# A graph block with experts: weight preparation in the first block, experts' weights behind index loads

## The chip, the cores and the metric

The kernel runs on one core of a Trainium2 chip. The metric is the device time of one execution in microseconds. The hand-written program gives TensorE (PE), VectorE (DVE), ScalarE (ACT), GpSimd (POOL) and SyncE (SP) their own instruction lists, which meet only at semaphores. SP, ACT and GpSimd also issue DMAs: SP's go through queue q1, ACT's through q10, GpSimd's through q0, and all run on the core's 16 DMA engines.

## The reference

One layer over a graph with 6250 nodes of 256 features and 100,000 edges sorted by destination, all in float32:

```python
def gat_conv(x, src, dst, W, a_src, a_dst, b):
    h = (x @ W).reshape(-1, H, C)
    alpha_s = einsum('nhc,hc->nh', h, a_src)
    alpha_d = einsum('nhc,hc->nh', h, a_dst)
    e = leaky_relu(alpha_s[src] + alpha_d[dst], 0.2)
    m = segment_max(e, dst)
    ex = exp(e - m[dst])
    alpha = ex / (segment_sum(ex, dst)[dst] + 1e-16)
    return segment_sum(h[src] * alpha[:, :, None], dst).reshape(-1, H * C) + b
xn = layernorm(x)
x = x + gat_conv(relu(gat_conv(xn, ...W1...)), ...W2...) + linear_attention(xn, Wqkv, Wout, bout)
x = x + experts(layernorm(x), gate_w, w1, w2, ...)      # 16 experts, the best 2 of each node
```

Self-loops are added to the edges. The attention normalises keys and values over each head's 64 features before their product, and its result is one 256 by 256 matrix applied to every node.

## The kernel before

The program is a row of stages, each with its own semaphores, ended by a barrier of all engines: `prepare_edges`, `project_inputs`, `bounds`, `maxima`, `gat_edges` (first layer), `bounds`, `maxima`, `gat_edges` (second layer), `order`, `experts`, `finish`. Nodes go in 49 tiles of 128, edges in 98 chunks of 1024 (8 per partition).

`prepare_edges` (L229) copies the list of sources to `srcp`, and loads the destinations twice: as `dst_i` (L274), where every partition takes eight neighbouring integers of each chunk, so 32 bytes at a time, and as `by_chunk_i` (L276), 97 whole chunks of 4 KB each on a partition of its own. VectorE waits for these loads (L303) and then makes from them, step by step (L304 to L356), the codes that say to which window and which node an edge belongs. SP stores the codes at L279.

`project_inputs` (L368) has two blocks. In the first, SP issues nine loads of weights (L399 to L407: W1, W2, four attention vectors broadcast to all partitions, the key and value weights of 1 MB, the query and output weights of 512 KB each); all add to one semaphore, and VectorE (L416) and TensorE (L437) wait for all nine. VectorE then appends the attention columns to W1 and W2 (L541, L542), copies six groups of four transposes that TensorE makes in one PSUM tile, `psW` (L424, L426), and takes the mean per head from the key and value weights (L431 to L433). In the second block x is loaded (L461), normalised, turned and multiplied with W1, tile by tile.

`gat_edges` (L761) is the edge stage. SP loads a chunk's sources (`idx`, three slots, L885) and its codes, broadcast to all partitions (`codes`, two slots, L889); GpSimd gathers the chunk's 1024 rows of the table in eight indirect DMAs into one of three slots (L931), once TensorE has added up what was in the slot (`added`, L929); VectorE makes the one-hot matrices (L971, L988), logits (L982 to L984) and scales the rows with ACT's exponentials (L995); TensorE adds up (L1215). `chunks` (L843) writes such a loop with an offset for each step; the code loads run one chunk ahead. In SP's list this gives: codes 0, idx 0, codes 1, idx 1, codes 2, idx 2. Codes 2 wait until VectorE has made the one-hot of chunk 0 (L888). At the start of the stage VectorE multiplies the self-loops' terms with their weights (L960), four long instructions. In the second layer ACT first issues three loads of four experts' weights each, 2 MB a load, into `w1` (L1162, L1163), which the later stages need (`weights_in`); the last four experts' come in `order`.

Of the kernel before, what the change touches and what calls it, by code (L numbers as in the profile page):

```python
# [25 lines left out]
P = 128  # L26
# [109 lines left out]
def build(nc, a, out):  # L136
# [15 lines left out]
    with ExitStack() as top:  # L152
# [27 lines left out]
        with ExitStack() as gnn:  # L180
# [26 lines left out]
            edges = (codes_d, partition, iota, acc, own, peak, parts, windows)  # L207
            stage(prepare_edges, a, srcp, codes_d, partition, ident, identb, ones, iota, eps, code, lower, upper, first_tile, passes)
# [19 lines left out]

def prepare_edges(nc, a, srcp, codes_d, partition, ident, identb, ones, iota, eps, code, lower, upper, first_tile, passes, sem):  # L229

# [3 lines left out]
    with ExitStack() as ctx:  # L234
        def sb(name, shape, dt=F32):
            return ctx.enter_context(nc.sbuf_tensor(name, shape, dt))
# [23 lines left out]
        count_i = sb("count_i", [1, 1], I32)  # L260
        base = sb("base", [P, 2, NC])
        ps = ctx.enter_context(nc.psum_tensor("pe_ps", [P, 512], F32))
        ps2 = ctx.enter_context(nc.psum_tensor("pe_ps2", [P, 512], F32))
        s = {n: sem("e_" + n) for n in ("filled", "loaded", "stored", "consts", "steps", "turned", "rowed", "spread", "tiled", "zeroed", "coded")}
        block = ctx.enter_context(nc.Block())
# [28 lines left out]
        def _(dve):  # L294
# [6 lines left out]
            dve.tensor_copy(partition[:], partition_i[:])  # L301
            dve.tensor_copy(identb[:], ident[:])
            dve.wait_ge(s["loaded"], 64)  # L303
            dve.tensor_copy(code[:], dst_i[:])  # L304
# [51 lines left out]
            chain.link(dve.scalar_tensor_tensor(code[:], code[:], SPREAD, residue[:], ALU.mult, ALU.add))  # L356

        @block.tensor
        def _(pe):
            pe.wait_ge(s["consts"], 1)  # L360
            pe.wait_ge(s["tiled"], 1)
# [6 lines left out]
def project_inputs(nc, a, xnT_d, table, ident, eps, acc, dtab, dotsT, wkvT, wq, woutT, wext1, sem):  # L368

    with ExitStack() as ctx:  # L370
        def sb(name, shape, dt=F32):
            return ctx.enter_context(nc.sbuf_tensor(name, shape, dt))
# [3 lines left out]

        wext = sb("wext0", [P, 2, HW])
        att = sb("att0", [P, 2, C])
        attw = sb("attw0", [P, 2, C])
        att1 = sb("att1", [P, 2, C])  # L380
        wkv = sb("wkv", [P, 8, C])
        wmean = sb("wmean", [P, 2 * MH])
        wout = sb("wout", [P, 2, MI])
        x = sb("x_in", [P, BUFS, C])
# [6 lines left out]
        psH = pb("psH", [P, 2, 512])  # L391
        psW = pb("psW", [P, 512])
        loaded, steps, turned, moved = sem("i_loaded"), sem("i_steps"), sem("i_turned"), sem("i_moved")
        first_block = ExitStack()
        block = first_block.enter_context(nc.Block())

        @block.sync
        def _(sp):
            sp.dma_start(wext[:, :, 0:C], a["L0_gnn_W1"].rearrange("(k p) n -> p k n", p=P)).then_inc(loaded, 16)  # L399
            sp.dma_start(att[:, 0, :], a["L0_gnn_att_src1"].rearrange("(o h) c -> o (h c)", o=1).to_broadcast([P, C])).then_inc(loaded, 16)  # L400
            sp.dma_start(att[:, 1, :], a["L0_gnn_att_dst1"].rearrange("(o h) c -> o (h c)", o=1).to_broadcast([P, C])).then_inc(loaded, 16)
            sp.dma_start(wext1[:, :, 0:C], a["L0_gnn_W2"].rearrange("(k p) n -> p k n", p=P)).then_inc(loaded, 16)
            sp.dma_start(att1[:, 0, :], a["L0_gnn_att_src2"].rearrange("(o h) c -> o (h c)", o=1).to_broadcast([P, C])).then_inc(loaded, 16)
            sp.dma_start(att1[:, 1, :], a["L0_gnn_att_dst2"].rearrange("(o h) c -> o (h c)", o=1).to_broadcast([P, C])).then_inc(loaded, 16)
            sp.dma_start(wkv[:], a["L0_mix_Wqkv"][MI:3 * MI, :].rearrange("(k p) c -> p k c", p=P)).then_inc(loaded, 16)
            sp.dma_start(wq, a["L0_mix_Wqkv"][0:MI, :].rearrange("(k p) c -> p k c", p=P)).then_inc(loaded, 16)
            sp.dma_start(wout[:], a["L0_mix_Wout"].rearrange("(k p) c -> p k c", p=P)).then_inc(loaded, 16)  # L407

        @block.vector
        def _(dve):  # L410
            chain = Chain(dve, steps)
            dve.memset(acc[:, NT:NT + 2, :], 0.0)
            dve.memset(acc[:, NT + 2, :], 1.0)
            dve.memset(dtab[:, NT:NT + 3, :], 0.0)
            dve.memset(dotsT[:], 0.0)
            dve.wait_ge(loaded, 144)  # L416
            attention_columns(dve, chain, wext, att, attw)
            attention_columns(dve, chain, wext1, att1, attw)

            for g in range(6):  # L420
                dve.wait_ge(turned, g + 1)
                if g < 4:
                    kc, q = g // 2, g % 2
                    dve.tensor_copy(wkvT[:, kc, q, :], psW[:, :]).then_inc(moved, 1)  # L424
                else:
                    dve.tensor_copy(woutT[:, :, (g - 4) * P:(g - 3) * P], psW[:, :].rearrange("p (k f) -> p k f", k=4)).then_inc(moved, 1)  # L426

            dve.wait_ge(moved, 6)
            for kc in range(2):
                w = wkvT[:, kc, :, :].rearrange("p a (g d) -> p (a g) d", d=MD)  # L430
                chain.link(dve.tensor_reduce(wmean[:], w, AX.X, ALU.add))  # L431
                chain.link(dve.tensor_scalar(wmean[:], wmean[:], 1.0 / MD, None, ALU.mult))
                chain.link(dve.tensor_tensor(w, w, wmean[:].rearrange("p (g d) -> p g d", d=1).to_broadcast([P, 2 * MH, MD]), ALU.subtract))  # L433

        @block.tensor
        def _(pe):
            pe.wait_ge(loaded, 144)  # L437
            for g in range(6):
                if g:
                    pe.wait_ge(moved, g)  # L440
                for j in range(4):
                    if g < 4:
                        kc, q = g // 2, g % 2
                        ins = pe.transpose(psW[:, j * P:(j + 1) * P], wkv[:, 4 * q + j, kc * P:(kc + 1) * P], ident[:])
                    else:
                        ins = pe.transpose(psW[:, j * P:(j + 1) * P], wout[:, g - 4, j * P:(j + 1) * P], ident[:])
                ins.then_inc(turned, 1)
# [5 lines left out]
        block2 = ctx.enter_context(nc.Block())  # L453

        @block2.sync
# [8 lines left out]
        @block2.gpsimd  # L464
        def _(pool):
# [5 lines left out]

        @block2.vector
        def _(dve):
# [17 lines left out]

        @block2.scalar
        def _(act):
# [22 lines left out]

        @block2.tensor
        def _(pe):
# [242 lines left out]
def gat_edges(nc, layer, srcp, table, codes_d, partition, iota, acc, own, peak, parts, windows, attention, last, sem):  # L761
# [5 lines left out]
    with ExitStack() as ctx:  # L767
# [337 lines left out]
        def _(act):  # L1105
# [19 lines left out]
            if attention:  # L1125
# [637 lines left out]
```

## Time and profile before

| | |
|---|---|
| median of 3 runs | 3288.85 us (3284.75 to 3294.06) |
| profiled execution | 3300.46 us |
| its span, first to last instruction | 3298.8 us |
| TensorE busy in the span | 2148.4 us (65%), mean granted clock 0.819 |
| GpSimd busy | 1932.8 us (59%) |
| VectorE busy | 1829.2 us (55%) |
| ACT busy | 931.4 us (28%) |
| DMA, over the span | 121 GB/s |

The profile is of one execution, which lasted a little longer than the median of the runs; 1.7 us of it lie outside the span. Shares of the whole span say little here, since the stages have different limits. Timeline rows give the start and the duration in microseconds, the engine (a q behind it, as in SPq, marks the engine's own issue of a DMA), the line, what is written and read, and in brackets how long the engine stood idle before, and what ended that. An issue's duration is the time that the engine needs to hand the transfer over, not that of the transfer.

### The profile page before, as it was taken

Reading aid. Unit: us, or ns where it says so; the run is one execution under the profiler, and the core shown is the slowest. Engines: PE = TensorE matmul, PEld = TensorE weight load, DVE = VectorE, ACT = ScalarE, POOL = GpSimd, SP = SyncE. Lnnn points to the kernel's source line nnn. Section 1 sums busy time; section 2 is a strip of 40 time slices with the busy share of each in tenths; the row PEclk is TensorE's granted clock in tenths of the full one; section 3 lists DMA queues with packets and bytes.
Section 4 is the critical chain, followed back from the end, with each engine's and each line's share of the span. In section 5 each row is a group of like instructions: output and inputs, shape, how many; then the busy total and the mean of one; then the engine's idle time right before and its main releaser. Section 6 shows DMA issues by size and latency. Waiting matters only on the chain. (4 is left out here: it accounts for less than half of the span.)

```text
span 3298.8 us, 50988 instructions
## 1 busy us (share of the span) xinstructions
PE 2148.4 (65%) x10263; PEld 1637.1 (50%) x10264; DVE 1829.2 (55%) x4382; ACT 931.4 (28%) x2254; POOL 1932.8 (59%) x1918
## 2 busy tenths in 40 slices
PE   0636666566667676645566665666666556999996
PEld 0424444344434454433444444444445445999994
DVE  4655555565555565564455554655555456555555
ACT  0412222222322223220122221222222123444445
POOL 0246666666666666617666666666666621666663
PEclk9967888788888788876777777777777767999998
DMA  2634444444444444425445454454454425555555
GB/s 55 190 107 117 116 121 118 117 116 124 116 120 122 116 122 119 114 93 147 126 130 139 127 137 124 132 136 127 128 135 128 126 69 155 102 101 105 102 97 168
DMA packets 273930, 399.38 MB, mean 121 GB/s; under 512 B 90593, under 2 KB 187256, under 8 KB 273850
## 3 DMA queue, kind: packets, MB, share of 16 engines
q0 software_dynamic: 101728, 251.76, 31.2%
q1 hardware_dynamic: 131417, 104.31, 11.7%
q10 hardware_dynamic: 40720, 42.61, 3.9%
q8 instruction: 21, 0.34, 0.0%
q14 instruction: 44, 0.35, 0.0%
HBM read 344.28 MB, written 54.62 MB: 121 GB/s over the span
## 5 line engine op out<-in xcount | busy, mean ns | idle before, releaser
L931 POOL DMA_INDIRECT gathered<-table,idx x1568 | 1581.8, 1009 | 830.3 <-issue 464.1
L1215 PE MATMUL psA_e<-gathered,hotf 128*128 128x260 f32 x3136 | 892.7, 445 | 109.9 <-issue 55.4
L1215 PEld LDWEIGHTS psA_e<-gathered,hotf 128*128 128x128 f32 x3136 | 706.8, 229 | 269.0 <-issue 131.7
L1112 ACT ACTIVATE gathered<-t_e 128x32 f32<-128x32 f32 x196 | 45.1, 230 | 1106.0 <-issue 603.8
L1003 DVE SCALAR_TENSOR_TENSOR acc<-psA_e,lower,acc 128x260 f32 x196 | 95.8, 489 | 284.1 <-issue 227.3
L1626 POOL DMA_INDIRECT moe_d<-xscaled,xtarget x113 | 179.2, 1586 | 124.7 <-DVE xtarget L1570 46.9
L988 DVE TENSOR_TENSOR hotf<-iota,code_r 128x1024 f32<-128x1024 bf16 x196 | 240.3, 1226 | 7.9 <-issue 7.9
L995 DVE TENSOR_TENSOR gathered<-gathered,psW_e 128x2048 f32<-128x2048 f32 x98 | 223.5, 2280 | 2.3 <-issue 2.3
L1598 PEld LDWEIGHTS xpsH<-xxT,w1e 128*128 128x128 f32 x1808 | 220.5, 193 | 6.2 <-ACT xxT L1527 0.4
L995 DVE TENSOR_TENSOR gathered<-gathered,psDW_e 128x2048 f32<-128x2048 f32 x98 | 223.4, 2279 | 0.0
L1607 PE MATMUL xpsO<-w,hidT 128*128 x904 | 217.4, 383 | 7.3 <-DVE hidT L1559 6.5
L1598 PE MATMUL xpsH<-xxT,w1e 128*128 128x128 f32 x1808 | 221.2, 276 | 0.0
L1207 PE MATMUL psDW_e<-dwin,hotT 128*128 128x24 bf16 x784 | 39.0, 176 | 234.5 <-DVE gathered L995 164.2
L1223 PE MATMUL psKV<-w 128*128 128x512 f32 x196 | 115.6, 719 | 109.0 <-ACT w L1132 89.9
L1559 DVE TENSOR_SCALAR hidT<-xpsH,b1T 128x128 f32<-128x128 f32 x452 | 127.3, 344 | 94.4 <-issue 43.5
L1207 PE MATMUL psD_e<-dwin,hotT 128*128 128x24 bf16 x784 | 41.6, 174 | 210.8 <-issue 119.1
L1607 PEld LDWEIGHTS xpsO<-w,hidT 128*128 128x128 f32 x904 | 163.0, 190 | 30.7 <-issue 12.6
L1207 PEld LDWEIGHTS psDW_e<-dwin,hotT 128*128 128x128 bf16 x784 | 33.9, 100 | 287.6 <-issue 256.8
L1229 PE MATMUL psKV<-w 128*128 128x512 f32 x196 | 138.7, 847 | 39.2 <-DVE w L1037 38.1
L1274 PE MATMUL psY<-mixM,w 128*128 128x256 f32 x196 | 70.3, 492 | 119.5 <-issue 55.5
L1207 PEld LDWEIGHTS psD_e<-dwin,hotT 128*128 128x128 bf16 x784 | 33.5, 97 | 226.7 <-issue 192.0
L982 DVE TENSOR_TENSOR z_e<-both_e,gathered 128x32 f32<-128x32 f32 x196 | 38.0, 194 | 184.8 <-DMA gathered<-table,idx 138.2
(314 smaller groups left out, 3252.3 us busy)
## 6 DMA issues: line engine op xcount, KB each, us to landing
codes<-codes_d SPq DMA_DIRECT2D x196, 256.0 KB
gathered<-table,idx POOLq DMA_INDIRECT x1568
w<-in_L_ffn_w ACTq DMA_DIRECT2D x8, 2048.0 KB
xb<-in_L_ffn_b SPq DMA_DIRECT2D x113, 128.0 KB
w<-xnT_d SPq DMA_DIRECT2D x98, 128.0 KB
table<-acc POOLq DMA_DIRECT2D x49, 130.0 KB, 2.7
table<-acc ACTq DMA_DIRECT2D x49, 130.0 KB
xnT_d<-xnT ACTq DMA_DIRECT2D x49, 128.0 KB, 1.8
```

The lines of the kernel that those rows point to most:

```text
L931: pool.indirect_dma_start(out=G[:, q, k, :], out_offset=None, in_=table, in_offset=bass.IndirectOffsetOnAxis(ap=idx[:, q, k:k + 1], axis=0 ...
L988: dve.tensor_tensor(hotf[:, q, :, :], iota[:].rearrange("p (k f) -> p k f", k=1).to_broadcast([P, KT, P]), code_r[:, ds(c * KT, KT)].rearr ...
L995: dve.tensor_tensor(f, f, w, ALU.mult).then_inc(s["scaled"], 1)
L1003: dve.scalar_tensor_tensor(into, psA[:, q, 0:GW], mask[:, ds(c, 1)], into, ALU.mult, ALU.add).then_inc(s["acc"], 1)
L1207: ins = pe.matmul(psD[:, 2 * k:2 * k + 2, :, :].rearrange("p g c h -> p (g c h)"), hotT[:, par, k, :], dwin[:, q, :], start=True, stop=True)
L1215: ins = pe.matmul(psA[:, q, 0:GW], hotf[:, q, k, :], G[:, q, k, :], start=(k == 0), stop=(k == KT - 1))
L1223: ins = pe.matmul(psKV[:, 1, :], xnT[b][:, kc * P:(kc + 1) * P], wkvT[:, kc, 1, :], start=(kc == 0), stop=(kc == 1))
L1229: ins = pe.matmul(psKV[:, 0, :], xnT[b][:, kc * P:(kc + 1) * P], wkvT[:, kc, 0, :], start=(kc == 0), stop=(kc == 1))
L1559: dve.tensor_scalar(hidT[:, q % 2, k * P:(k + 1) * P], psH[:, q % 2, k * P:(k + 1) * P], b1T[:, ds(e, 1), k:k + 1].rearrange("p o k -> p ( ...
L1598: ins = pe.matmul(psH[:, q % 2, k * P:(k + 1) * P], w1e[:, q % 2, kc, k * P:(k + 1) * P], xT[:, q % 2, kc, :], start=(kc == 0), stop=(kc = ...
L1607: ins = pe.matmul(psO[:, q % 2, 0:C], hidT[:, q % 2, k * P:(k + 1) * P], w2[:, ds(e, 1), k, :].rearrange("p o f -> p (o f)"), start=(k == ...
L1626: pool.indirect_dma_start(out=moe_d, out_offset=bass.IndirectOffsetOnAxis(ap=target[:, q % 2:q % 2 + 1], axis=0), in_=scaled[:, q % 2, :], ...
```

## The change

The nine loads, VectorE's preparation of the weights and TensorE's transposes move from the first block of `project_inputs` into the only block of `prepare_edges`, which is called `prepare` now. ACT issues the loads; it had nothing to do in that block. On VectorE the preparation stands ahead of the wait for the edges' loads, on TensorE ahead of the transposes for the edges. `project_inputs` keeps its second block alone; `wext0` is allocated around both stages. In the second layer's `gat_edges` ACT waits for the codes of chunk 1 and for `idx` of slot 2 before it issues the experts' weights.

```diff
-            stage(prepare_edges, a, srcp, codes_d, ...)
+            attention_weights = (wkvT, wq, woutT, wext1)
...
-            stage(project_inputs, a, xnT_d, table[0], ident, eps, acc, dtab, dotsT, wkvT, wq, woutT, wext1)
+            with ExitStack() as first:
+                wext0 = sb("wext0", [P, 2, HW], F32, first)
+                stage(prepare, a, srcp, codes_d, ..., acc, dtab, dotsT, wext0, attention_weights)
+                stage(project_inputs, a, xnT_d, table[0], ident, eps, acc, dtab, wext0)
...
             dve.tensor_copy(identb[:], ident[:])
+            weights = Chain(dve, s["w_steps"])
+            dve.memset(acc[:, NT:NT + 2, :], 0.0)
+            dve.memset(acc[:, NT + 2, :], 1.0)
+            dve.memset(dtab[:, NT:NT + 3, :], 0.0)
+            dve.memset(dotsT[:], 0.0)
+            dve.wait_ge(s["w_loaded"], 144)
+            attention_columns(dve, weights, wext, att, attw)
+            attention_columns(dve, weights, wext1, att1, attw)
+
+            for g in range(6):
+                dve.wait_ge(s["w_turned"], g + 1)
...
+            dve.wait_ge(s["w_moved"], 6)
+            for kc in range(2):
...
             dve.wait_ge(s["loaded"], 64)
             dve.tensor_copy(code[:], dst_i[:])
...
+        @block.scalar
+        def _(act):
+            act.dma_start(wext[:, :, 0:C], a["L0_gnn_W1"].rearrange("(k p) n -> p k n", p=P)).then_inc(s["w_loaded"], 16)
...
+            act.dma_start(wout[:], a["L0_mix_Wout"].rearrange("(k p) c -> p k c", p=P)).then_inc(s["w_loaded"], 16)
+
         @block.tensor
         def _(pe):
             pe.wait_ge(s["consts"], 1)
+            pe.wait_ge(s["w_loaded"], 144)
+            for g in range(6):
...
+                ins.then_inc(s["w_turned"], 1)
             pe.wait_ge(s["tiled"], 1)
...
-        first_block = ExitStack()
-        block = first_block.enter_context(nc.Block())
...
-        first_block.close()
...
             else:
+                act.wait_ge(s["codes_in1"], 16)
+                act.wait_ge(s["idx_in2"], 16)
                 for e in range(0, NX - 4, 4):
                     act.dma_start(w1[:, e:e + 4, :, :], ...).then_inc(weights_in, 16)
```

## Rows read from the trace of the kernel before

**Rows 1.** The view of windows, core 0; columns: stretch, length, busy us (instructions) by engine, granted clock, DMA share, GB/s.

```profile
0.00:93.40 93.40, 8.29 (x28) 4.91 (x29) 41.47 (x84) 0.02 (x1) 1.16 (x11) 1.00 0.23 49
93.40:186.00 92.60, 67.01 (x294) 43.52 (x294) 53.80 (x196) 50.74 (x197) 26.69 (x49) 0.99 0.68 209
```

**Rows 2.** Timeline, 0 to 93.5: start, us, engine, line, operation, [idle before <-releaser].

```profile
0.97 0.67 SPq L271 DMA_DIRECT2D srcp<-in_src  x1
...
29.00 0.57 DVE L304 CAST code<-dst_i 128x784 f32<-128x784 int32 x1 [25.71 <-DMA by_chunk_i<-in_dst]
...
53.24 0.40 SPq L399 DMA_DIRECT2D wext<-in_L_gnn_W  x1
...
70.02 0.43 DVE L541 TENSOR_TENSOR attw<-wext,att 128x256 f32<-128x256 f32 x1 [15.27 <-DMA wout<-in_L_mix_Wout]
...
91.74 1.22 DVE L433 TENSOR_TENSOR w<-w,wmean 128x1024 f32<-128x1024 f32 x1
93.44 0.34 SPq L461 DMA_DIRECT2D x_in<-in_x  x1
```

**Rows 3.** Waits of GpSimd in the second edge stage: us in total, times, longest us.

```profile
POOL gathered L931 <- remote: 161.5, 45, 4.8
...
POOL gathered L931 <- PE psA_e L1215: 10.6, 11, 3.4
```

**Rows 4.** DMA view of 1:29, 18:29 and 53:70, in this order: packets, MB, share of 16 engines.

```profile
DMA packets 12717, 1.20 MB, mean 43 GB/s; under 512 B 12603, under 2 KB 12603, under 8 KB 12701
...
q1 hardware_dynamic: 12717, 1.20, 33.5%
...
q1 hardware_dynamic: 68, 0.27, 6.1%
...
q1 hardware_dynamic: 2960, 3.15, 69.7%
```

**Rows 5.** DMA view of 1476:1478: SP's queue q1, ACT's queue q10.

```profile
q10 hardware_dynamic: 278, 0.54, 70.7%
q1 hardware_dynamic: 274, 0.24, 35.8%
```

**Rows 6.** Timeline at the start of the first and of the second edge stage.

```profile
204.46 0.37 SPq L885 DMA_DIRECT2D idx<-srcp  x1
...
208.34 3.32 POOL L931 DMA_INDIRECT gathered<-table,idx  x1 [5.12 <-issue]
211.96 2.97 POOL L931 DMA_INDIRECT gathered<-table,idx  x1 [0.30 <-issue]
...
1467.15 7.49 ACTq L1163 DMA_DIRECT2D w<-in_L_ffn_w  x3
...
1467.54 13.43 DVE L960 TENSOR_TENSOR acc<-acc 128x3136 f32<-128x3136 f32 x4 [0.43 <-ACT acc L1108]
...
1470.90 0.48 SPq L885 DMA_DIRECT2D idx<-srcp  x1
...
1475.73 1.28 ACT L1112 ACT_TABLE_LOAD   x1 [8.22 <-issue]
1479.20 2.65 POOL L931 DMA_INDIRECT gathered<-table,idx  x1 [11.83 <-DMA idx<-srcp]
...
1483.44 0.95 POOL L931 DMA_INDIRECT gathered<-table,idx  x1 [0.31 <-issue]
...
1483.90 0.36 SPq L885 DMA_DIRECT2D idx<-srcp  x1
...
1498.82 5.18 PE L1215 MATMUL psA_e<-gathered,hotf 128*128 128x260 f32 x16 [12.67 <-DVE gathered L995]
...
1515.63 0.95 POOL L931 DMA_INDIRECT gathered<-table,idx  x1 [3.57 <-remote]
```

**Rows 7.** Windows with the matmuls of L1215 alone: stretch, length, busy us (instructions), clock, DMA share, GB/s.

```profile
228.00:237.00 9.00, 6.09 (x16) 4.57 (x16) 0.59 0.49 142
2021.00:2026.00 5.00, 3.67 (x16) 3.04 (x16) 1.00 0.77 208
```

More of the change, by code:

```diff
@@ L212, in build @@
             combine = (a, xnT_d, xf_d, moe_d, ident, ones, eps, mixM, hot, extra, w1, weights_in, ahead)
[L213 removed]
+            with ExitStack() as first:
+                wext0 = sb("wext0", [P, 2, HW], F32, first)
+                stage(prepare, a, srcp, codes_d, partition, ident, identb, ones, iota, eps, code, lower, upper, first_tile, passes,
+                      acc, dtab, dotsT, wext0, attention_weights)
+                stage(project_inputs, a, xnT_d, table[0], ident, eps, acc, dtab, wext0)
             stage(bounds, 0, ident, ones, acc, dtab, own, peak, parts, wide)
@@ L261, in prepare_edges @@
         base = sb("base", [P, 2, NC])
+        wkvT, wq, woutT, wext1 = attention_weights
+        att = sb("att0", [P, 2, C])
+        attw = sb("attw0", [P, 2, C])
+        att1 = sb("att1", [P, 2, C])
+        wkv = sb("wkv", [P, 8, C])
+        wmean = sb("wmean", [P, 2 * MH])
+        wout = sb("wout", [P, 2, MI])
         ps = ctx.enter_context(nc.psum_tensor("pe_ps", [P, 512], F32))
         ps2 = ctx.enter_context(nc.psum_tensor("pe_ps2", [P, 512], F32))
-        s = {n: sem("e_" + n) for n in ("filled", "loaded", "stored", "consts", "steps", "turned", "rowed", "spread", "tiled", "zeroed", "coded")}
+        psW = ctx.enter_context(nc.psum_tensor("pe_psW", [P, 512], F32))
+        s = {n: sem("e_" + n) for n in ("filled", "loaded", "stored", "consts", "steps", "turned", "rowed", "spread", "tiled", "zeroed", "coded",
+                                         "w_loaded", "w_steps", "w_turned", "w_moved")}
         block = ctx.enter_context(nc.Block())
@@ L302, in _ @@
             dve.tensor_copy(identb[:], ident[:])
+            weights = Chain(dve, s["w_steps"])
[8 more added lines that the diff above has]
+                dve.wait_ge(s["w_turned"], g + 1)
+                if g < 4:
+                    kc, q = g // 2, g % 2
+                    dve.tensor_copy(wkvT[:, kc, q, :], psW[:, :]).then_inc(s["w_moved"], 1)
+                else:
+                    dve.tensor_copy(woutT[:, :, (g - 4) * P:(g - 3) * P], psW[:, :].rearrange("p (k f) -> p k f", k=4)).then_inc(s["w_moved"], 1)
+            dve.wait_ge(s["w_moved"], 6)
+            for kc in range(2):
+                w = wkvT[:, kc, :, :].rearrange("p a (g d) -> p (a g) d", d=MD)
+                weights.link(dve.tensor_reduce(wmean[:], w, AX.X, ALU.add))
+                weights.link(dve.tensor_scalar(wmean[:], wmean[:], 1.0 / MD, None, ALU.mult))
+                weights.link(dve.tensor_tensor(w, w, wmean[:].rearrange("p (g d) -> p g d", d=1).to_broadcast([P, 2 * MH, MD]), ALU.subtract))
             dve.wait_ge(s["loaded"], 64)
@@ L360, in _ @@
             pe.wait_ge(s["consts"], 1)
+            pe.wait_ge(s["w_loaded"], 144)
+            for g in range(6):
+                if g:
+                    pe.wait_ge(s["w_moved"], g)
+                for j in range(4):
+                    if g < 4:
+                        kc, q = g // 2, g % 2
+                        ins = pe.transpose(psW[:, j * P:(j + 1) * P], wkv[:, 4 * q + j, kc * P:(kc + 1) * P], ident[:])
+                    else:
+                        ins = pe.transpose(psW[:, j * P:(j + 1) * P], wout[:, g - 4, j * P:(j + 1) * P], ident[:])
+                ins.then_inc(s["w_turned"], 1)
             pe.wait_ge(s["tiled"], 1)
@@ L365, in _, with project_inputs @@
             pe.matmul(ps2[:, 0:2 * NC], ones[0:1, :], spread_row[:].rearrange("o a k -> o (a k)"), start=True, stop=True).then_inc(s["spread"], 1)
-def project_inputs(nc, a, xnT_d, table, ident, eps, acc, dtab, dotsT, wkvT, wq, woutT, wext1, sem):
+def project_inputs(nc, a, xnT_d, table, ident, eps, acc, dtab, wext, sem):
     with ExitStack() as ctx:
@@ L409, in _ @@
[L409 to L447, printed above, removed]
@@ L449, in project_inputs @@
-        first_block.close()
         s = {n: sem("i_" + n) for n in ("x_in0", "x_in1", "x_in2", "x_in3", "xT_out0", "xT_out1", "xT_out2", "xT_out3", "xT_ps", "xT", "h_ps", "h_out",
                                         "h_stored", "stats", "root", "xn", "first", "norm", "tick")}
-        block2 = ctx.enter_context(nc.Block())
-        @block2.sync
+        block = ctx.enter_context(nc.Block())
+        @block.sync
         def _(sp):
@@ L462, in _ @@
             tiles(sp, (0, load))
-        @block2.gpsimd
+        @block.gpsimd
         def _(pool):
@@ L470, in _ @@
             pool.wait_ge(s["h_stored"], 16 * NT)
-        @block2.vector
+        @block.vector
         def _(dve):
@@ L490, in _ @@
             tiles(dve, (1, normalise), (0, stats))
-        @block2.scalar
+        @block.scalar
         def _(act):
@@ L515, in _ @@
                 act.wait_ge(s[f"xT_out{q}"], 16 * uses(q))
-        @block2.tensor
+        @block.tensor
         def _(pe):
```

31 lines of the change are left out of this document (9 added, 22 removed).

## The prediction

> **What bounds the kernel now.** I read three things in this order: the stretches by stage, the timeline of the two places that the diff touches, and the DMA view of the same moments.
>
> The first 93.4 us are preparation. In that stretch VectorE is busy 41.47 us, TensorE 8.29 us, and the DMA engines 0.23 of the time; no unit is full [rows 1]. It is a chain of waits and VectorE work in two turns [rows 2]. VectorE first waits 25.71 us for the edge list (the load `by_chunk_i`), then works on the edges from 29.00 on. After that and the change of stage SP issues the weights' loads from 53.24, so the edges' work and the change of stage are 24.24 us together; VectorE waits 15.27 us for the last of them and works from 70.02 to 92.96 (91.74 + 1.22) on the weights: 22.94 us. The first load of x is issued at 93.44. So the stretch is wait, work, change of stage, wait, work. Neither half needs anything of the other.
>
> In the second edge stage GpSimd sets the pace. It issues 98 x 8 = 784 gathers, a gather takes 0.95 us and 0.31 us of issue ahead of it (the one at 1483.44) [rows 6], 988 us in all. To this come 161.5 us of what the profile calls remote, while it idles only 10.6 us for TensorE's `psA_e` [rows 3]. That is 1160 us of a stage of some 1200. What moves GpSimd's gathers forward moves the stage forward; what delays the other engines costs nothing until GpSimd has to wait for them.
>
> **Part 1: the weights' preparation.** Removed is nothing but one wait and one block boundary; the nine loads, the VectorE work and the 24 transposes stay. The loads move from SP's queue (53.24) to ACT's, which is empty; they can be issued from about 1.0, when SP issues its own first load [rows 2]. VectorE's order becomes: weights first (wait for all nine loads, then 22.94 us), then the wait for the edges, then the 24.24 us of the edges' work and the change of stage. The 0.48 us of the block boundary between 92.96 and 93.44 go away.
>
> So the first load of x is issued at T + 22.94 + 24.24 = T + 47.18, where T is the landing of the last weight, provided the edges have landed by T + 22.94. Everything hangs on T.
>
> Alone the nine loads took 70.02 - 53.24 = 16.8 us from first issue to landing [rows 2], of which the 16 engines were busy 0.697 x 17 = 11.85 us [rows 4]. From 1.0 this gives T = 17.8, the earliest that I allow. Now they share the engines with SP's loads. Those were busy 0.335 x 28 = 9.4 us of all engines. In it are 15.3 us of a single engine: `by_chunk_i` has 97 rows, and the 68 packets of the stretch 18 to 29 took 0.061 x 11 x 16 / 68 = 158 ns each, one after another [rows 4]. That is 15.3 / 16 = 0.95 of the 9.4, so the rest is 8.4 us on every engine, nearly all of it the 12,603 small packets, `dst_i`'s, for the stretch holds 12,717 in all. If the weights wait for all of that, T = 26.2. If on the one engine they wait for `by_chunk_i` as well, T = 41.4, the latest. No row shows this pair of transfers at once. The nearest is ACT's and SP's queue side by side at 1476 to 1478: 278 packets of the one and 274 of the other, so they take turns packet by packet [rows 5]. By turns each of the weights' 2960 / 16 = 185 packets per engine waits for one small packet of 8.4 x 16 / 12,603 = 11 ns, 2 us in all: T = 19.8. But the small packets are far from the size of those in rows 5, so I take about the middle of 19.8 and 26.2: **T = 23**.
>
> The edges then land at most 11.85 us later than at 29.00, at 40.9. VectorE would ask for them at 23 + 22.94 = 45.9, so this wait is hidden with 5 us to spare; without that cover it would cost what is over. TensorE's waits for the weights stand ahead of its two edge transposes, which come long after. VectorE's four memsets run in the wait for T. The store of the codes on SP keeps its place inside the edges' work.
>
> The first load of x is issued at 23 + 47.18 = 70.2 instead of 93.44: **23.3 us** gained, with 28.5 for T = 17.8, 14.2 for T = 32, and 4.9 for T = 41.4. After it comes the same stage as before, so the whole rest moves by that much.
>
> The Trainium skill, "DMA: Bandwidth & Descriptors", section "Queues, rings and completion order", says that a DMA engine changes between queues only at the end of a packet, which may hold up to 64 descriptors. The records of `dst_i` would then go by in bundles and the weights get less than every second turn; T would be about 26 and the result 3 us later than mine. Rows 5 can't decide, as both sides there have large records.
>
> **Part 2: the experts' weights.** ACT issued three loads of 2 MB at 1467.15, and the issue took 7.49 us. The first index load was issued at 1470.90, and the first gather began at 1479.20, 8.3 us later. In the first edge stage, without such loads, it was 204.46 to 208.34: 3.9 us [rows 6]. So GpSimd could begin at 1474.8. But the first gathers run beside VectorE's 13.43 us of L960, and there they take 3.32 and 2.97 us, the second 3.6 us after the first, in place of 0.95 [rows 6]. L960 ends at 1480.97. The gathers would begin at 1474.8, 1478.4 and, with the step of 3.3 us that the second's 2.97 gives, at 1481.7; before, the third began at 1483.44. **Gain 1.7 us**, for the third and all behind it. Bounds: 4.4 us if none of it is eaten by the slow gathers.
>
> The new waits are ahead of the three issues on ACT. The later of them is for `idx` slot 2, a load that SP issues only behind VectorE's first one-hot, at 1483.90 [rows 6]. So ACT issues from about 1486.5 to 1494, and then comes its table load, which now stands at 1475.73, 1.1 us behind the issue, and takes 1.28 us; queued behind are its first exponentials. They could start at about 1496.4. Now they and the scaling behind them are over when `add` begins at 1498.82; so they would come some 1 to 2 us later. GpSimd needs this chain only for its 25th gather: the first `add` ended at 1504.0 and the 25th began at 1515.63 after 3.57 us of remote, so 8 us of slack stand against at most 2 + 1.7 us. I cost it at nothing; if the slack were gone it would be up to 3 us. The loads also run beside gathers for some 25 us. That happens now too, with the gather at 1483.44 still at 0.95 us. Between a gain of 4.4 and a loss of 3 I take 1.7, the one with rows.
>
> **Sum.** 23.3 + 1.7 = 25.0 us. The profiled execution took 3300.46 us (span 3298.8 and 1.7 around it) and would become 3275.5. The median of the runs is 3288.85, 11.6 below; the saved pieces are waits and issues at fixed times, so I take the same 25 off: **3263.9 us**.
>
> **Rivals.**
> - *The weights come late* because the edge loads hold them, on the one engine with `by_chunk_i` above all. For: that engine is the last of both. Against: turns packet by packet [rows 5]. T = 32 to 41 gives 15.9 to 6.6 us, so 3273 to 3282. Chance 0.23.
> - *The second part doesn't do what it says.* The wait is not for the first index loads but for the third, so ACT is held up 19 us and then blocked by its own issue; the exponentials come late and eat the gain. Against: the slack of 8 us. Part 1 stays: 3288.85 - 23.3 + 0 to 3 = 3265.6 to 3268.6. Chance 0.17.
> - *TensorE's clock, the slower side.* The projection pass runs from 93.4 to 186 at a granted 0.99, the 2.4 GHz level, though TensorE did little before [rows 1]. Moved forward it could find 1.2 GHz. The same 16 matmuls took 6.09 us in a stretch at 0.59 and 3.67 at 1.00 [rows 7], a factor of 1.66; on 67.01 us of TensorE work that is 44 us if nothing hides it, so 3264 + 44 = 3308. It decides from 35 us on, when the pass stays low for four fifths of its length. Against: the record shows 1.00 over the whole first stretch, in which TensorE worked 8.29 of 93.4 us. Chance 0.04. The Trainium skill, "TensorE: Matmul & The Clock Gate", section "What's actually happening", names the low level as the default; the trace does not agree, with 1.00 over the first 93.4 us.
>
> **How the numbers follow.** Forecast 0.52, the rivals 0.23, 0.17 and 0.04, and 0.04 for what I don't see. A measurement of this kernel can tell about 0.3% from no change, 9.9 us; the runs before spread over 9.3. The forecast and the second rival are faster by more; of the first, about three quarters. Faster 0.87, within 0.3% 0.09, slower 0.04. The range goes from 28.5 + 4.4 gained (3256) and the spread of the runs below it, 3251, up to the first rival's end, 3281.
>
> **What would show it.** L541's first instruction begins near 23 and waits for the weights; L304 follows L433 without a wait; SP's first load of x stands near 70; the first gather of the second edge stage stands 8.3 less 3.9 us nearer to the stage's start, and the third 1.7 us nearer; ACT's issue comes after SP's third index load. I am wrong if L541 starts past 30, if L304 waits for `by_chunk_i`, or if the pass over x takes longer than 92.6 us.

## The result, and the profile after

The changed kernel takes 0.9915 of the time of the kernel before, with an interval of 0.9899 to 0.9931: 3255.16 us against 3281.9 us, medians of six runs each. The ratio is 27.9 us on 3281.9 (22.6 to 33.1); 25.0 were predicted. The predicted time was 3263.9 us. Of the 8.7 us between it and the measured one, 7.0 come from the kernel before, whose median was 3288.85 when the prediction was made. The profiled execution of the changed kernel took 3252.82 us, its span is 3251.2.

The two profiled spans differ by 47.6 us, much more than the runs do. This table takes the starts of the stages from both timelines (the first load of x; GpSimd's first instruction in each edge stage and in `order`):

| start of | before | after | earlier by |
|---|---|---|---|
| first load of x | 93.44 | 67.94 | 25.5 |
| first edge stage | 202.15 | 176.80 | 25.4 |
| second edge stage | 1465.71 | 1430.41 | 35.3 |
| `order` | 2719.24 | 2670.46 | 48.8 |
| end | 3298.8 | 3251.2 | 47.6 |

The first 25.4 us stand where the change is. The next 9.9 arise in the first edge stage, which the change doesn't touch, and 13.5 in the second. The experiments tell how much of that other executions of the same kernels show without the change.

The first stretch of the changed kernel, from its timeline (columns as in [rows 2]):

```profile
0.97 0.43 ACTq L398 DMA_DIRECT2D wext<-in_L_gnn_W  x1
...
3.98 17.85 SPq L289 DMA_DIRECT2D dst_i<-in_dst  x1
...
20.69 0.43 DVE L536 TENSOR_TENSOR attw<-wext,att 128x256 f32<-128x256 f32 x1 [16.01 <-DMA wout<-in_L_mix_Wout]
...
21.88 0.26 SPq L290 DMA_DIRECT2D by_chunk_i<-in_dst  x1
...
42.41 1.23 DVE L339 TENSOR_TENSOR w<-w,wmean 128x1024 f32<-128x1024 f32 x1
...
43.67 0.57 DVE L342 CAST code<-dst_i 128x784 f32<-128x784 int32 x1
...
67.94 0.83 SPq L456 DMA_DIRECT2D x_in<-in_x  x2
```

Three things are to be seen. The weights have landed at 20.69, the T of the prediction. The edges' work follows the weights' at once: L342, the old L304, has no wait in brackets where it had 25.71 us [rows 2]. And SP's issue at L289 takes 17.85 us, so that `by_chunk_i` is issued at 21.88: the weights hold the edge loads back far more than they are held back themselves. In held_edges, below, where the weights have landed before, the same issue takes 6.53 us.

The view of windows, over the new first stretch and the pass over x (columns as in [rows 1]):

```profile
0.00:67.90 67.90, 8.27 (x28) 4.88 (x29) 41.46 (x84) 0.02 (x1) 1.16 (x11) 1.00 0.33 67
67.90:160.00 92.10, 66.98 (x294) 43.33 (x294) 53.80 (x196) 49.90 (x197) 26.71 (x49) 1.00 0.70 210
```

VectorE does the same 41.46 us of work, in 67.9 us instead of 93.4. The pass over x lasts as long as before and keeps the granted clock of 1.00.

The start of the second edge stage, which begins at 1430.41 (to compare with [rows 6], where it began at 1465.71):

```profile
1435.06 0.37 SPq L880 DMA_DIRECT2D idx<-srcp  x1
...
1438.87 1.02 POOL L926 DMA_INDIRECT gathered<-table,idx  x1 [6.79 <-DMA idx<-srcp]
1440.19 3.00 POOL L926 DMA_INDIRECT gathered<-table,idx  x1 [0.30 <-issue]
1443.49 3.00 POOL L926 DMA_INDIRECT gathered<-table,idx  x1 [0.30 <-issue]
...
1446.80 0.94 POOL L926 DMA_INDIRECT gathered<-table,idx  x1 [0.30 <-issue]
...
1451.85 7.50 ACTq L1160 DMA_DIRECT2D w<-in_L_ffn_w  x3
...
1458.34 0.19 DVE L977 TENSOR_TENSOR z_e<-both_e,gathered 128x32 f32<-128x32 f32 x1 [7.99 <-DMA gathered<-table,idx]
...
1460.43 1.28 ACT L1107 ACT_TABLE_LOAD   x1 [28.22 <-issue]
...
1461.73 0.23 ACT L1107 ACTIVATE gathered<-t_e 128x32 f32<-128x32 f32 x1
```

The first gather comes 3.8 us behind the index load instead of 8.3. The fourth begins 16.4 us after the stage's start; before it was the one behind 1483.44, at 19.0. So 2.6 us are gained there. The experts' weights are issued 21.4 us after the start, and the logits (from 1458.34 on) wait for ACT's table load: the first exponentials come 31.3 us after the start, and came at 29.6.

### The profile page after: what moved, and what is told of

It reads as the page before. It is cut to its first block and busy times, and to the rows that moved or that the text cites. A ratio compares the mean times of both kernels' runs of the same rounds, so it can differ in the third digit from the quotient of the medians.

```text
span 3251.2 us, 50978 instructions
## 1 busy us (share of the span) xinstructions
PE 2138.4 (66%) x10263; PEld 1632.7 (50%) x10264; DVE 1829.3 (56%) x4382; ACT 931.8 (29%) x2254; POOL 1934.7 (60%) x1918
## 3 DMA queue, kind: packets, MB, share of 16 engines
q0 software_dynamic: 101728, 251.76, 31.3%
## 5 line engine op out<-in xcount | busy, mean ns | idle before, releaser
L1212 PE MATMUL psA_e<-gathered,hotf 128*128 128x260 f32 x3136 | 871.8, 437 | 93.8 <-issue 59.2
L1212 PEld LDWEIGHTS psA_e<-gathered,hotf 128*128 128x128 f32 x3136 | 692.3, 224 | 244.4 <-issue 115.6
L1226 PE MATMUL psKV<-w 128*128 128x512 f32 x196 | 158.8, 956 | 41.6 <-DVE w L1032 40.1
L1220 PE MATMUL psKV<-w 128*128 128x512 f32 x196 | 115.4, 718 | 67.9 <-ACT w L1127 41.2
L1614 POOL DMA_INDIRECT xx<-xf_d,xsource x113 | 111.4, 986 | 40.9 <-issue 33.0
```

Source lines behind the costliest of these rows:

```text
L1212: ins = pe.matmul(psA[:, q, 0:GW], hotf[:, q, k, :], G[:, q, k, :], start=(k == 0), stop=(k == KT - 1))
L1220: ins = pe.matmul(psKV[:, 1, :], xnT[b][:, kc * P:(kc + 1) * P], wkvT[:, kc, 1, :], start=(kc == 0), stop=(kc == 1))
L1226: ins = pe.matmul(psKV[:, 0, :], xnT[b][:, kc * P:(kc + 1) * P], wkvT[:, kc, 0, :], start=(kc == 0), stop=(kc == 1))
L1614: pool.indirect_dma_start(out=x[:, q, :], out_offset=None, in_=xf_d, in_offset=bass.IndirectOffsetOnAxis(ap=source[:, q:q + 1], axis=0)).t ...
```

## Experiments

The runs were made in three sessions, each with runs of the kernel before beside them. The times of the kernel before differ from session to session (3002.7, 3289.0 and 3260.7 us), so only ratios to the kernel before of the same session and the places inside a stage are compared. The numbers in brackets behind a ratio are its 95% interval.

### The change in halves

part1_only:

```diff
-                act.wait_ge(s["codes_in1"], 16)
-                act.wait_ge(s["idx_in2"], 16)
```

> The changed kernel without its two new waits on ACT, so only the weights' preparation is moved. Theory: part 1 is worth what the first load of x moves, 93.44 to 67.94 = 25.5 us; this kernel should take 25.5 us less than the kernel before (ratio 0.992), and its first load of x should again be issued at 67.9, the first gather of the second edge stage 13.5 us after that stage's start as before. Rival: in the profiled pair the two edge stages were also 10.0 and 13.5 us shorter than before; if that comes from the change, and here from part 2, this kernel gains clearly less than the changed one, some 12 us less.

Measured: 0.9924 (0.9908 to 0.994), 2982.57 us against 3002.72. The first load of x is issued at 67.8.

part2_only, on the kernel before:

```diff
+                act.wait_ge(s["codes_in1"], 16)
+                act.wait_ge(s["idx_in2"], 16)
                 for e in range(0, NX - 4, 4):
```

> The kernel before with the two new waits on ACT alone. Theory: GpSimd's gathers stand 2 to 3 us nearer to the start of the second edge stage (in the changed kernel the fourth began 16.39 us after it, in the kernel before 18.98), and nothing eats it: 2.5 us faster, ratio 0.9992, hardly to be told from 1. Rival A: the exponentials come 2 us late and eat it: ratio 1.000. Rival B: the 13.5 us by which the second edge stage was shorter in the profiled pair are its doing: ratio 0.996.

Measured: 0.9987 (0.9976 to 0.9998), 2999.42 us.

both_again is the changed kernel as it is.

> The changed kernel once more, beside its two halves. Theory: 25.5 + 2.5 = 28 us below the kernel before (ratio 0.9915), and the length of each edge stage differs by several us between two executions of the same kernel, so that the 47.6 us between the two profiled executions are 28 of the change and 20 of chance. Rival: the edge stages repeat within 2 us in every execution of the changed kernel, and are shorter than those before by 10 us each time.

Measured: 0.9897 (0.988 to 0.9914), 2972.75 us, where 0.9915 was expected.

The first half is worth 0.0076 x 3002.7 = 23 us (18 to 28), the second 4 (0.6 to 7), and the product of the two ratios, 0.9911, lies inside the interval of the whole. The rival by which part 2 alone shortens the second edge stage by 13.5 us falls: its own interval ends at 7. So does the one by which the late exponentials eat the gain, though only just. On top of part 1 the second half looks larger: part1_only lies 9.8 us above both_again by the medians, where 2.5 were expected and 12 by its rival. The intervals of these two overlap, so the runs leave open whether part 2 is worth 3 us or some more. In these profiles the second edge stage lasted 1093.0 us without the new waits and 1086.6 and 1088.3 with them, one execution each.

The first edge stage lasted 1120.2 us in part1_only, 1119.9 in both_again and 1121.1 in part2_only, which has the first half of the kernel before. So the change doesn't shorten that stage, and the 9.9 us of the table are not its doing.

What differs between part1_only and both_again at that start, first part1_only, then both_again, GpSimd's timeline; the stages begin at 1296.8 and 1297.0:

```profile
1310.19 2.74 POOL L926 DMA_INDIRECT gathered<-table,idx  x1 [11.74 <-DMA idx<-srcp]
```

```profile
1305.35 1.14 POOL L926 DMA_INDIRECT gathered<-table,idx  x1 [6.68 <-DMA idx<-srcp]
```

The gather that began 13.4 us after the start begins at 8.3, and the wait for the index load shrinks from 11.74 to 6.68 us. Further on the gain grows: part1_only begins its 4th, 25th and 32nd gather 19.0, 46.6 and 56.1 us after the start, both_again 16.4, 43.8 and 52.6. That is 2.6, 2.8 and 3.5 us. What adds the last part isn't shown.

These two profiles also settle what the late exponentials cost. They come 32.1 us after the start in both_again, and GpSimd's 25th gather, the first that needs the chain behind them, follows the 24th after 0.30 us of issue. GpSimd's waits for TensorE over the whole execution, first part1_only, then both_again:

```profile
POOL gathered L926 <- PE psA_e L1210: 11.9, 39, 0.3
```

```profile
POOL gathered L926 <- PE psA_e L1212: 13.4, 44, 0.3
```

None is longer than 0.3 us. The exponentials cost GpSimd nothing.

### The kernel before once more

> The kernel before, profiled beside the next ones. The first profile of it had 95 pauses of GpSimd put down to remote, 318 us, and took 3300 us; the four kernels run after it had none of them, and the kernel before took 3002.7 us beside them. Theory: those pauses belong to the chip or its hour, not to the kernel, so here the profile shows none and edge stages of 1121 and 1090 us in place of 1264 and 1253, and the same 93 us before the first load of x. Rival: the pauses belong to this kernel's queue and come again.

Measured: 3289.35 us, in a session whose runs of the kernel before had a median of 3288.97. The theory that this profile would show none falls, as the pauses are back. GpSimd's waits, first in before_again, then in both_again from the session before:

```profile
POOL gathered L931 <- issue: 461.8, 1454, 5.3
POOL gathered L931 <- remote: 294.6, 92, 4.8
```

```profile
POOL gathered L926 <- issue: 466.7, 1515, 5.6
```

All four kernels of the first session have no such row, and both kernels of the first profiled pair and all eight of the second and third have 266 to 318 us of it. So it goes with the session and not with the kernel, and that much of the theory stands. What the pauses are, the profile doesn't show. Some of them seem to be counted under TensorE's name: without pauses no wait for `psA_e` is longer than 0.3 us, with them there are some of 3 to 5, as at the 25th gather of the changed kernel (3.00 us).

The run answers the question of chance, too. The same kernel's edge stages lasted 1263.6 and 1253.5 us in its first profile and 1249.1 and 1255.6 in this one: a difference of 14 us in the first of them, without any change. The 9.9 us of the first edge stage in the table are within that. Of the second, the changed kernel's first profile has 1240.0, and held_edges, which has the new waits as well, has 1253.1. So most of its 13.5 us is the same kind of difference. The wander goes with the pauses: the first edge stages of the four kernels without them lie within 2.7 us.

### The order on VectorE, and when the edges land

edges_first puts VectorE's and TensorE's work for the edges ahead of that for the weights:

```diff
-            dve.wait_ge(s["w_loaded"], 144)
-            attention_columns(dve, weights, wext, att, attw)
...
             dve.wait_ge(s["loaded"], 64)
...
             chain.link(dve.scalar_tensor_tensor(code[:], code[:], SPREAD, residue[:], ALU.mult, ALU.add))
+            dve.wait_ge(s["w_loaded"], 144)
+            attention_columns(dve, weights, wext, att, attw)
...
```

> The changed kernel with the edges' work ahead of the weights' on VectorE and TensorE; the loads are as they are. VectorE then shows when the edges land, L, and the order's worth. Theory: by_chunk_i is issued at 22, behind the small packets, and moves 97 x 158 ns = 15.3 us on one engine, so L = 38; the first load of x comes at 38 + 24.24 + 22.94 = 85, 17 us later than the changed kernel's 67.9, and only 8 us earlier than before. Rival: the edges land as before, near 29, and the order is worth 8 us (first load of x at 76).

Measured, from its timeline:

```profile
39.36 0.57 DVE L323 CAST code<-dst_i 128x784 f32<-128x784 int32 x1 [34.67 <-DMA by_chunk_i<-in_dst]
...
86.60 1.77 SPq L455 DMA_DIRECT2D x_in<-in_x  x4
```

The edges land at 39.36, and the first load of x comes at 86.6, 18.7 us behind the changed kernel's. So the order is the larger part of the change as its loads are issued: the same loads beside each other, with the edges first, give 6.8 us of the 25.5. Of the 18.7 us, 10.4 are there because the edges land at 39.36 beside the weights and landed at 29.00 [rows 2] without them; an issue that let them land earlier would make the order worth less. In the changed kernel VectorE asks for the edges at 43.67, 4.3 us after this landing.

### What the contention costs

held_edges:

```diff
+            sp.wait_ge(s["w_loaded"], 144)
             sp.dma_start(dst_i[:, 0:FULL * KT].rearrange("p (k t) -> p k t", t=KT), whole).then_inc(s["loaded"], 16)
```

> The changed kernel with SP waiting for the nine weights before it issues the edges' loads, so that the weights have the engines for themselves (but for srcp). It prices the contention in T. Theory: the weights land at 17.8 in place of 20.7, the edges 28 - 3.5 = 25 us behind them at 43; VectorE ends the weights at 40.7, waits 2 us, and the first load of x comes at 43 + 24.2 = 67, within 1 us of the changed kernel: contention costs T 3 us and gives the edges 5. Rival, from the rule that a DMA engine serves 64 small descriptors in a bundle: contention costs the weights more than that, and T falls to 15 or below.

Measured, from its timeline:

```profile
18.72 0.42 DVE L537 TENSOR_TENSOR attw<-wext,att 128x256 f32<-128x256 f32 x1 [14.04 <-DMA wout<-in_L_mix_Wout]
...
43.52 0.57 DVE L343 CAST code<-dst_i 128x784 f32<-128x784 int32 x1 [1.86 <-DMA by_chunk_i<-in_dst]
...
67.79 22.53 SPq L457 DMA_DIRECT2D x_in<-in_x  x15
```

Without the edge loads T is 18.72 instead of 20.69: the contention costs 2.0 us, and the rival that had T at 15 or below falls. Then the edges are late, at 43.52, VectorE waits 1.86 us for them, and the first load of x is where it was. So the changed kernel loses nothing against one that holds the edge loads back. The other order, the edge loads ahead of the weights, no run shows.

The DMA view of the changed kernel from 11 to 17, then from 14 to 15 and from 15 to 16, where ACT's queue has most to move; SP's q1 has the small packets and ACT's q10 the weights:

```profile
q10 hardware_dynamic: 1554, 1.66, 90.2%
q1 hardware_dynamic: 2133, 0.07, 23.8%
...
q10 hardware_dynamic: 294, 0.30, 100.2%
q1 hardware_dynamic: 294, 0.01, 25.4%
...
q10 hardware_dynamic: 254, 0.30, 99.7%
q1 hardware_dynamic: 254, 0.01, 22.2%
```

Over the six us that is 1.4 small packets to a large one, and in the two single us it is one to one, the turns that gave T = 19.8 in the prediction. In held_edges, without small packets, the weights move 337 and 276 packets in these two us, so the small ones take 43 and 22 from them. Before and after this stretch the small ones are many more, 3012 to 257 from 8 to 11 and 5760 to 239 from 17 to 21. From 8 to 11 the weights lose little by it, for they move 271 packets there in held_edges; from 17 on they are running out. These rows don't decide. By the rule of the Trainium skill that I weighed there ("DMA: Bandwidth & Descriptors", section "Queues, rings and completion order"), bundles of up to 64 small ones would stand against a few large ones. The rows from 14 to 16 don't show it, and the 2.0 us don't either. Bundles of equal numbers on both sides would give the same counts as turns of one, and these rows can't tell the two apart.

### VectorE's work in the wait for the weights

early_columns lets each set of attention columns wait for its own three loads, and cuts the load of 97 rows:

```diff
-            sp.dma_start(by_chunk_i[0:FULL, :], ...).then_inc(s["loaded"], 16)
+            sp.dma_start(by_chunk_i[0:96, :], ...).then_inc(s["loaded"], 16)
+            sp.dma_start(by_chunk_i[96:FULL, :], ...).then_inc(s["loaded"], 16)
...
-            dve.wait_ge(s["w_loaded"], 144)
+            dve.wait_ge(s["w_one"], 48)
             attention_columns(dve, weights, wext, att, attw)
+            dve.wait_ge(s["w_two"], 48)
             attention_columns(dve, weights, wext1, att1, attw)
```

> The changed kernel, with VectorE's attention columns waiting only for the three loads that each needs (two new semaphores) in place of all nine, and the edges' by_chunk_i load split into 96 rows and 1, so that it runs on all DMA engines. Theory: VectorE stood idle from 4.7 to 20.69, and 7.3 us of attention columns fit in there if W1 and its two vectors land before 13; then VectorE starts the copies at 20.7 and the first load of x is issued at 67.9 - 7.3 = 60.6, 7 us (0.2%) faster than the changed kernel. Rival: the broadcast attention vectors land late because dst_i's small packets take the engines from 5 on, W1's three loads land at 15 or later, and the gain is 3 us or less; or the by_chunk_i load, spread over all engines, holds the weights up and T moves past 21 by as much.

Measured: 0.9885 (0.9868 to 0.9902) beside the changed kernel's 0.9897 (0.988 to 0.9914). From its timeline:

```profile
8.16 0.42 DVE L538 TENSOR_TENSOR attw<-wext,att 128x256 f32<-128x256 f32 x1 [3.47 <-DMA att<-in_L_gnn_att_dst]
...
13.42 0.43 DVE L538 TENSOR_TENSOR attw<-wext,att 128x256 f32<-128x256 f32 x1 [1.64 <-DMA att<-in_L_gnn_att_dst]
...
21.89 0.69 DVE L332 COPY w<-pe_psW 128x512 f32<-128x512 f32 x1 [4.86 <-PE pe_psW L420]
```

Both sets fit ahead of the copies, and the first load of x is issued at 61.9, against 67.6 in both_again: 5.7 us instead of 7.3, as the copies now wait for TensorE's first transposes. The split of the edge load has a share in it: VectorE asks for the edges at 37.56, ahead of the 39.36 at which the unsplit load landed in edges_first, and doesn't wait. In 96 rows and 1 the load is issued at 22.23, and the DMA engines have nothing left to do from 24.75 on. The time is 4.8 us lower by the medians, within the intervals. In the third session it was repeated.

> early_columns once more, beside the changed kernel and pieces. Theory: first load of x at 62, 5.7 us before the changed kernel's, and so 5.7 us (0.17%) faster. Rival: the edge stages give it back, and the two can't be told apart.

Measured: 0.9896 (0.9875 to 0.9916), 3228.09 us, where the changed kernel had 3225.41. The first load of x stood at 62.6 against 68.6. So the 6 us at the start stand in both profiles, and that they reach the end is not shown: one session has them, the other doesn't, and neither can resolve them.

### Who holds the first gathers

pieces is early_columns with L960 in halves:

```diff
             for h in range(H):
-                f = acc[:, 0:NT, h * CH:(h + 1) * CH]
-                dve.tensor_tensor(f, f, ...).then_inc(s["own_terms"], 1)
-            dve.wait_ge(s["own_terms"], H)
+                for lo, hi in ((0, NT // 2), (NT // 2, NT)):
+                    f = acc[:, lo:hi, h * CH:(h + 1) * CH]
+                    dve.tensor_tensor(f, f, ...).then_inc(s["own_terms"], 1)
+            dve.wait_ge(s["own_terms"], 2 * H)
```

> The kernel early_columns with each of VectorE's four instructions of L960 (3.42 us each) cut in two. Theory: a gather that GpSimd begins beside L960 is held until the running VectorE instruction ends (in the changed kernel 1.02, 3.00, 3.00 us, one gather to an instruction), so halves of 1.7 us let a gather through every 1.7 us: in the second edge stage the fourth gather begins 2 us earlier (14.4 after the stage's start, was 16.4), in the first 3 us, and the kernel gains about 4 us over early_columns, ratio to the kernel before 0.987. Rival: GpSimd is slowed by the share of time that VectorE holds the memory port, not by the instruction, and nothing changes but 0.3 us of overhead.

Measured: 0.9894 (0.987 to 0.9918) in the second session, 0.987 was expected. Without early_columns beside it this tells little, so it was repeated.

> The kernel pieces once more, beside early_columns. In its profile the seventh gather of the first edge stage began 16.7 us after the stage's start, where the fourth had stood, so three gathers or 3.7 us are gained there, and one or two in the second stage. Theory: GpSimd sets the pace of both stages, so it is 4 to 6 us faster than early_columns. Rival: what is gained at the start is given back where GpSimd waits for TensorE (43.9 us on psA_e in its profile on a chip with pauses, 33.7 in the kernel before), and it is no faster.

Measured: 0.9864 (0.9842 to 0.9885), 3217.52 us; beside it early_again had 0.9896 and the changed kernel 0.9888. GpSimd's first gathers of the second edge stage, early_again (stage's start 1406.1) and then pieces_again (1404.1):

```profile
1414.70 4.21 POOL L928 DMA_INDIRECT gathered<-table,idx  x1 [6.94 <-DMA idx<-srcp]
1419.22 3.00 POOL L928 DMA_INDIRECT gathered<-table,idx  x1 [0.30 <-issue]
1422.52 0.94 POOL L928 DMA_INDIRECT gathered<-table,idx  x1 [0.30 <-issue]
```

```profile
1412.74 1.00 POOL L928 DMA_INDIRECT gathered<-table,idx  x1 [6.95 <-DMA idx<-srcp]
1414.05 1.33 POOL L928 DMA_INDIRECT gathered<-table,idx  x1 [0.30 <-issue]
1415.68 1.41 POOL L928 DMA_INDIRECT gathered<-table,idx  x1 [0.30 <-issue]
1417.39 1.36 POOL L928 DMA_INDIRECT gathered<-table,idx  x1 [0.30 <-issue]
1419.06 1.43 POOL L928 DMA_INDIRECT gathered<-table,idx  x1 [0.31 <-issue]
1420.79 0.95 POOL L928 DMA_INDIRECT gathered<-table,idx  x1 [0.30 <-issue]
```

With VectorE's instructions of 3.4 us a gather comes every 3.3 us; with those of 1.7 us (13.71 us for eight) every 1.7 us. Each gather that is held ends 0.8 to 1.0 us behind the end of one of VectorE's instructions, about the time that it takes alone: VectorE's in pieces_again end at 1406.0 + n x 1.71, so at 1412.8, 1414.6, 1416.3, 1418.0 and 1419.7, and the gathers at 1413.74, 1415.38, 1417.09, 1418.75 and 1420.49. So a gather is held by the instruction that runs, and one gets through for each, at both lengths. The third gather of early_again begins 16.4 us after the start; pieces_again has begun its sixth at 16.7. This bears out the theory, and the rival of a shared rate falls. The Trainium skill, "SBUF — State Buffer", section "Who interferes with whom", says that a VectorE instruction with both inputs in SBUF contends with GpSimd instructions that read SBUF; these rows agree, with 0.95 us alone and 3.00 to 4.21 us beside it. pieces_again is 10.6 us faster than early_again by the medians and 7.9 faster than the changed kernel, the fastest of its session; the intervals of the ratios (0.9842 to 0.9885 and, for the changed kernel, 0.9866 to 0.991) still overlap.

### Which loads ACT should wait for

first_index, beside both_third, the changed kernel:

```diff
-                act.wait_ge(s["codes_in1"], 16)
-                act.wait_ge(s["idx_in2"], 16)
+                act.wait_ge(s["codes_in0"], 16)
+                act.wait_ge(s["idx_in1"], 16)
```

> The changed kernel a third time, as the base of the next three on the same chip. Theory: 0.990 to 0.9915 of the kernel before, as twice already, whether or not the chip has GpSimd's pauses, since these come between gathers in both kernels alike.

Measured: 0.9888 (0.9866 to 0.991), 3225.41 us, a little below the 0.990 that was expected at the least. The first gather of the second edge stage took 3.97 us here, held as told above: it began 0.4 us later after the stage's start than in the first profile, just behind the start of one of VectorE's instructions (1424.0), where it had begun just ahead of one. So the third began at 16.4 us as the fourth does there, and part 2 gained 1.3 us at the start instead of 2.6.

> The changed kernel with ACT waiting for the codes of chunk 0 and the index load of chunk 1 in place of codes 1 and idx slot 2: the loads that SP issues before VectorE's first one-hot. Theory: ACT issues the experts' weights 8 to 9 us after the stage's start in place of 21.5, is done by 17, and its first exponentials come when the logits do (28.8 in place of 31.3 to 32.1 after the stage's start); but the weights now run beside the first gathers, which land 2 us later (first z_e at 29 to 30). GpSimd doesn't wait for either, as it has 8 us of slack at its 25th gather, so the time is that of the changed kernel within 2 us. Rival: the late exponentials do hold GpSimd at its 25th gather (in the profiled changed kernel it waited 3.00 us for psA_e there), and this kernel is 2 to 3 us faster.

Measured: 0.9909 (0.9889 to 0.993), 3231.68 us. ACT issues at 8.6 us after the stage's start, the first exponentials come at 28.3 instead of 31.8, and nothing is faster for it. The rival finds no support, as both_again without pauses has shown already: the exponentials' delay is hidden, as the prediction costed it. Whether the 6 us by which it is slower are real can't be told from these intervals.

## Why the prediction was right

**The chain** was right in each link. First load of x = T + 47.18: with the measured 20.69 that gives 67.87, and it stands at 67.94. The cover of the edges' load was predicted as 5 us and is 4.3. The following stage moved by the whole amount, and its granted clock stayed at 1.00, so the slower rival did not come. The Trainium skill, "TensorE: Matmul & The Clock Gate", section "What's actually happening", names the low level as the default; these rows again don't show it, with 1.00 over the first 67.9 us, in which TensorE worked 8.27.

**T** was mis-sized: I took 23, it is 20.69. The term in it is the contention, 5.2 us in my T, which measured 2.0 (20.69 - 18.72). The base was off the other way: without the edge loads the weights land at 18.72, and I took 17.8. The bound that went turn by turn gave just 2.0 for the contention; I had moved away from it towards the case of waiting for all small packets. The rival of late weights was for the same reason no danger. I had the direction wrong in it: the small packets yield, SP's issue grows from 6.55 to 17.85 us, and the edge loads pay.

**Part 2** was right in its mechanism and its hidden costs. The index load to first gather was 3.8 us (3.9 forecast), ACT's issue came 21.4 us after the stage's start, the exponentials 1.7 us later (1 to 2 forecast), and the profile of both_again shows that they cost nothing. Mis-sized was the gain, 1.7 us against 2.6 at the fourth gather in the first profile and 1.3 in both_third; part2_only gives 4 (0.6 to 7) by its runs. I gave the first gather the 3.32 us of the first edge stage; it lasts until 0.8 to 1.0 us behind the end of VectorE's instruction, so from 1.0 to 4.2 us in these profiles. The stage lasts 1253.5 us, not some 1200, which the sum doesn't use.

**The sum**, 25.0 forecast, is 25.5 + 2.6 = 28.1 by the trace and 27.9 (22.6 to 33.1) by the runs. It agrees, though by their ratios both_again and both_third (0.9897 and 0.9888) gain 31 and 37 us, 3 to 8 more than the trace explains. If that is more than noise, it isn't found here; the growth of part 2's gain by the 32nd gather is the one trace of it.

**The range**, 3251 to 3281, held with 3255.16, near its lower end mostly because the kernel before was 7.0 us faster than when I predicted, which is no merit of the forecast. Its upper end should have been 3282, where the first rival ends. My argument for taking the same saving off the median was sound, but the comparison of two profiled executions would have misled by 20 us: in sessions with pauses the edge stages differ by up to 14 us between executions of the same kernel.

## What to carry to other kernels

When two chains of "load, then one engine's work" don't need each other, issue both loads at once and order the work by which load lands first: here the order gave 18.7 of 25.5 us, and the rest of the change 6.8. Where small and large packets meet on the DMA engines, look for who pays: here it was the queue with the many small ones, and with it whatever SP was to issue next. And compare stages before spans: the difference of two profiled executions was 47.6 us, of which 28 can be put down to the change.

## What the runs showed of the hardware

- GpSimd's pauses that the profile calls remote, about 3 us each and 90 to 97 in an execution, were there in two sessions and in the first profiles, and in none of the four kernels of another session. The kernel before took 3289.0 and 3260.7 us in the ones and 3002.7 in the other: 8 to 9% of the time, more than this change and all its variants together. Two sessions reported the same chip, one with the pauses and one without. What they are stays open.
- A gather by GpSimd beside a long VectorE instruction on two SBUF operands is held until that instruction's end and takes its own time then: 0.95 us alone, 1.3 to 1.4 us beside pieces of 1.7 us, up to 4.21 beside pieces of 3.4.
- Beside each other, the queue of 32-byte packets and that of the weights moved equal numbers while ACT's had most to move (294 and 294, 254 and 254 in a us), and the issue of the small load takes 17.85 us in place of 6.55.
- A load of 97 rows runs on one DMA engine, 158 ns for a row of 4 KB, and stays at that when 15 engines are free [rows 4].
